# Two chained attentions on one core: other PSUM banks for the first attention's products, the next image's group statistics and several evictions moved in the written-out order, and two casts moved from VectorE to ScalarE

## Time and profile before

| | |
|---|---|
| median of 3 runs (lowest to highest) | 1849.27 us (1845.56 to 1850.44) |
| the profiled execution's own time | 1847.24 us |
| its span, first to last instruction | 1845.3 us |
| granted clock of TensorE, mean | 0.996 |
| PE / PEld busy | 95% / 86% |
| DVE / ACT / POOL busy | 76% / 51% / 41% |
| transfers | 169.67 MB, 92 GB/s over the span |

### The profile page before, as it was taken

The page is one execution under the profiler, slowest core; times in us unless marked ns, Lnnn a source line. Parts: engine busy times, 40 slices in busy tenths (PEclk is TensorE's granted clock), DMA queues, the critical chain, the costliest instruction groups (busy, mean ns, idle before and its releaser), DMA issues.

```text
span 1845.3 us, 34579 instructions
## 1 busy us (share of the span) xinstructions
PE 1760.7 (95%) x11810; PEld 1594.0 (86%) x11810; DVE 1403.4 (76%) x2596; ACT 937.6 (51%) x1476; POOL 754.1 (41%) x1334
## 2 busy tenths in 40 slices
PE   7999999999999999999999999999999999999997
PEld 6898888988889888898988989888898888988887
DVE  5778867787687877868778687786878868787675
ACT  3645545455463554635547354464545546456462
POOL 0442715327162361724617145271542715327161
PEclk9999999999999999999999999999999999999999
DMA  3404134051330504306042150422404134051330
GB/s 121 139 24 149 58 101 127 23 169 36 114 114 29 173 25 125 102 34 193 0 143 84 57 171 3 146 78 73 155 23 148 57 98 129 23 171 34 94 113 24
DMA packets 108575, 169.67 MB, mean 92 GB/s; under 512 B 12928, under 2 KB 79872, under 8 KB 108544
## 3 DMA queue, kind: packets, MB, share of 16 engines
q1 hardware_dynamic: 108544, 169.27, 29.0%
HBM read 85.33 MB, written 83.89 MB: 92 GB/s over the span
## 4 chain that ended last, share of the span: by engine, by line
PE 42%; issue 24%; POOL 21%; DVE 6%; ACT 4%; DMA 2%; POOLq 1%; SPq 1%; DVEq 0%; ACTq 0%
PE wide L368 12%; PE narrow L368 5%; POOL prob L1279 4%; PE wide L470 4%; PE wide L472 3%; PE wide L471 3%; PE narrow L470 3%; POOL ln_r L1247 3%; PE narrow L472 3%; PE narrow L471 3%; POOL sq_root L1261 2%; POOL ln_shift L1249 2%; PE turn L423 2%; PE turn L564 2%; PE turn L555 1%
## 5 line engine op out<-in xcount | busy, mean ns | idle before, releaser
L368 PE MATMUL wide<-xn_hi,prob 128*128 128x512 f32 x1024 | 304.9, 399 | 0.3 <-ACT expo L727 0.3
L1244 POOL TENSOR_TENSOR ln_v<-ln_mv,ln_eps 128x2 f32<-128x2 f32 (+2 forms) x128 | 39.2, 307 | 586.5 <-DVE ln_mv L1011 335.5
L761 ACT ACTIVATE ln<-tok,ln_shift,ln_r 128x256 f32<-128x256 f32 x128 | 68.4, 592 | 308.1 <-POOL ln_shift L1249 308.1
L368 PEld LDWEIGHTS wide<-xn_hi,prob 128*128 128x128 f32 x1024 | 185.5, 188 | 39.1 <-ACT expo L727 0.7
L727 ACT ACTIVATE expo<-wide,neg_max 128x1024 f32<-128x1024 f32 x128 | 142.1, 1110 | 136.2 <-DVE neg_max L983 136.2
L470 PE MATMUL narrow<-prob 128*128 128x256 f32 x640 | 188.6, 295 | 21.7 <-DVE tok L1006 18.6
L734 ACT ACTIVATE prob<-e_back 128x1024 fp32r<-128x1024 f32 x128 | 135.2, 1056 | 127.1 <-DMA e_back<-e_scratch 123.4
L990 DVE STREAM_TRANSPOSE x_norm<-expo 128x1024 f32<-128x1024 f32 x128 | 158.9, 1242 | 42.8 <-ACT expo L727 38.3
L471 PE MATMUL narrow<-prob 128*128 128x256 f32 x640 | 181.5, 284 | 0.0
L472 PE MATMUL narrow<-prob 128*128 128x256 f32 x640 | 181.4, 283 | 0.0
L1289 POOL TENSOR_TENSOR carrier_p<-ones 128x1 f32<-128x1 f32 x60 | 11.6, 193 | 415.5 <-DVE y_sb L1059 413.0
(11 more groups left out here) (182 smaller groups left out, 5392.8 us busy)
## 6 DMA issues: line engine op xcount, KB each, us to landing
e_scratch<-x_norm SPq DMA_DIRECT2D x128, 512.0 KB, 3.0
e_back<-e_scratch SPq DMA_DIRECT2D x512, 128.0 KB, 3.1
x_raw<-in_x SPq DMA_DIRECT2D x32, 512.0 KB, 3.9
out<-y_sb SPq DMA_DIRECT2D x32, 512.0 KB, 3.8
tok<-in_L_conv_qkv_w SPq DMA_DIRECT2D x1, 768.0 KB, 6.7
ln<-in_L_conv_proj_w SPq DMA_DIRECT2D x1, 256.0 KB, 6.8
ln<-in_L_ffn_weight SPq DMA_DIRECT2D x1, 256.0 KB, 3.9
out_bias<-in_L_conv_proj_b SPq DMA_DIRECT2D x1, 128.0 KB, 3.7
```

The costliest lines, as they stand in the source:

```text
L368: mm = pe.matmul(o, lhsT, r, start=first and i == 0, stop=last and i == len(parts) - 1)
L761: act.activation(ln2[:, n], tok[:, n], ACT.Identity, bias=ln2_shift[:, n:n + 1], scale=ln2_r[:, n:n + 1]).then_inc(ln2_made, 1)
```

## The change

The first attention's products no longer share one bank: blocks 0 to 3 go to narrow0, narrow1, narrow0 and the upper half of wide0, and the waits follow the banks. The group norm's two small products move from the turn tile to narrow0. On PE, `group_means` and `group_vars` move from the middle of the first attention to behind `turn_e2(2)` and `turn_e2(3)`, `scores1(7)`, `turn_cos(0)` and `product1(6)`, `product1(7)` move. On DVE, the two `gn_sums` move from the first attention to before and after `residual1(7)`, and `residual1`, `cosT_lo`, `e1T_lo`, `output` change places. On ACT, `exp2`, `cosT_hi`, `layer_norm1` change places; on POOL, `value_lo(1)` and `gn_coefficients` move back. The casts of the last row block of the second attention (two of 128x512 per image) are made by ACT behind the exponentials instead of by DVE. The number of matmuls, transfers and of all other operations stays.

```
-        out1 = [narrow[0]] * 4 + [turn[:, 0:BANK], narrow[0], wide[0][:, BANK:N], wide[1][:, BANK:N]]
-        gn_up = turn[:, BANK:BANK + KC]
+        out1 = [narrow[0], narrow[1], narrow[0], wide[0][:, BANK:N],
+                turn[:, 0:BANK], narrow[0], wide[0][:, BANK:N], wide[1][:, BANK:N]]
+        gn_up = narrow[0][:, 0:KC]
...
             def product1(b, n):
                 if n == 0:
                     pe.wait_ge(v_made, 4 * b + 4)
-                elif n < 4:
-                    pe.wait_ge(t1_made, NT * b + n)
-                elif n == 5:
-                    pe.wait_ge(t1_made, NT * b + 4)
+                elif n == 2:
+                    pe.wait_ge(t1_made, NT * b + 1)
+                elif n == 3:
+                    pe.wait_ge(e1_made, NT * b + 7)
+                elif n in (5, 6):
+                    pe.wait_ge(t1_made, NT * b + n - 2)
...
+                else:
+                    pe.wait_ge(t1_made, NT * b + 2)
...
                 product1(b, 2)
+                scores1(b, 7)
+                turn_cos(b, 0)
+                product1(b, 3)
...
-                if more:
-                    group_means(b + 1)
-                scores1(b, 7)
-                turn_cos(b, 0)
-                product1(b, 3)
                 product1(b, 4)
                 scores2(b, 0)
                 scores2(b, 1)
-                if more:
-                    group_vars(b + 1)
                 product1(b, 5)
+                product1(b, 6)
                 turn_cos(b, 1)
-                product1(b, 6)
-                if more:
-                    pe.wait_ge(gn_var, b + 2)
                 turn_e2(b, 1)
+                product1(b, 7)
                 scores2(b, 2)
-                product1(b, 7)
                 turn_cos(b, 2)
                 scores2(b, 3)
                 turn_e2(b, 2)
+                if more:
+                    pe.wait_ge(t1_made, NT * b + 6)
+                    group_means(b + 1)
                 scores2(b, 4)
                 turn_cos(b, 3)
                 turn_e2(b, 3)
+                if more:
+                    group_vars(b + 1)
                 scores2(b, 5)
+                turn_e2(b, 4)
                 turn_cos(b, 4)
-                turn_e2(b, 4)
...
                 turn_e2(b, 6)
+                if more:
+                    pe.wait_ge(gn_var, b + 2)
...
+            def e2_last_hi(b, u):
+                J, c0, c1 = PARTS[u]
+                act.wait_ge(e2_made, NP * b + u + 1)
+                act.activation(prob[:, 0, J, c0:c1], expo[:, J % DEEP, c0:c1], ACT.Copy).then_inc(p_last_hi_made, 1)
...
                 e1T_hi(b, 6)
-                layer_norm1(b, 1)
                 exp2(b, 0)
                 exp2(b, 1)
+                layer_norm1(b, 1)
                 unit_rows(b, 1)
-                cosT_hi(b, 1)
                 e1T_hi(b, 7)
                 layer_norm1(b, 2)
-                exp2(b, 2)
+                cosT_hi(b, 1)
                 unit_rows(b, 2)
                 layer_norm1(b, 3)
+                exp2(b, 2)
                 cosT_hi(b, 2)
                 unit_rows(b, 3)
                 exp2(b, 3)
                 layer_norm1(b, 4)
+                unit_rows(b, 4)
                 cosT_hi(b, 3)
-                unit_rows(b, 4)
...
                 exp2(b, 7)
+                e2_last_hi(b, 7)
                 exp2(b, 8)
+                e2_last_hi(b, 8)
...
                 residual1(b, 0)
-                if more:
-                    gn_sums(b + 1, 0)
                 row_max(b, 5)
                 e1T_lo(b, 2)
-                if f is not None:
-                    output(f, 1)
                 e1_turn(b, 5)
                 residual1(b, 1)
-                if more:
-                    gn_sums(b + 1, 1)
+                if f is not None:
+                    output(f, 1)
                 row_max(b, 6)
                 e1T_lo(b, 3)
                 e1_turn(b, 6)
-                residual1(b, 2)
                 row_max(b, 7)
                 e1T_lo(b, 4)
                 e1_turn(b, 7)
                 cosT_lo(b, 0)
+                e1T_lo(b, 5)
+                residual1(b, 2)
                 residual1(b, 3)
-                e1T_lo(b, 5)
-                if more:
-                    gn_deviation(b + 1)
+                e1T_lo(b, 6)
                 residual1(b, 4)
-                e1T_lo(b, 6)
-                if more:
-                    gn_variance(b + 1)
                 e2_hi(b, 0)
                 e2_hi(b, 1)
                 residual1(b, 5)
-                cosT_lo(b, 1)
                 e1T_lo(b, 7)
                 residual1(b, 6)
+                cosT_lo(b, 1)
+                if more:
+                    gn_sums(b + 1, 0)
                 e2T_parts(b, 1)
+                residual1(b, 7)
+                if more:
+                    gn_sums(b + 1, 1)
                 e2_hi(b, 2)
-                residual1(b, 7)
                 cosT_lo(b, 2)
                 e2T_parts(b, 2)
+                if more:
+                    gn_deviation(b + 1)
                 e2_hi(b, 3)
                 cosT_lo(b, 3)
                 e2T_parts(b, 3)
+                if more:
+                    gn_variance(b + 1)
                 e2_hi(b, 4)
+                e2T_parts(b, 4)
                 cosT_lo(b, 4)
-                e2T_parts(b, 4)
...
                 e2_hi(b, 6)
-                e2_hi(b, 7)
                 e2_last_lo(b, 7)
                 e2T_parts(b, 6)
-                e2_hi(b, 8)
                 e2_last_lo(b, 8)
...
-                value_lo(b, 1)
                 layer_norm1(b, 2)
                 lengths(b, 2)
+                value_lo(b, 1)
...
                 value_lo(b, 4)
-                if more:
-                    gn_coefficients(b + 1)
                 e2_lo(b, 4)
                 e2_lo(b, 5)
                 e2_lo(b, 6)
+                if more:
+                    gn_coefficients(b + 1)
```

More of the change, by code:

```diff
@@ L241, in build @@
         p_made = sem("p_made")
+        p_last_hi_made = sem("p_last_hi_made")
         p_last_made = sem("p_last_made")
@@ L1026, in e2_last_lo @@
                 J, c0, c1 = PARTS[u]
-                dve.wait_ge(p_hi_made, NP * b + u + 1)
+                dve.wait_ge(p_last_hi_made, 2 * b + u - NT + 2)
                 dve.tensor_sub(prob[:, 1, J, c0:c1], expo[:, J % DEEP, c0:c1],
@@ L1111, in front @@
                 residual1(b, 0)
-                if more:
-                    gn_sums(b + 1, 0)
                 row_max(b, 5)
                 e1T_lo(b, 2)
+                e1_turn(b, 5)
+                residual1(b, 1)
                 if f is not None:
                     output(f, 1)
-                e1_turn(b, 5)
-                residual1(b, 1)
-                if more:
-                    gn_sums(b + 1, 1)
                 row_max(b, 6)
@@ L1277, in e2_lo @@
                 row = slice(0, (J + 1) * P)
-                pool.wait_ge(p_hi_made, NP * b + J + 1)
+                pool.wait_ge(p_hi_made, (NT - 1) * b + J + 1)
                 pool.tensor_sub(prob[:, 1, J, row], expo[:, J % DEEP, row], prob[:, 0, J, row].bitcast(F32)
```

## The result

The changed kernel takes 1840.45 us (median of 8 runs, 1836.0 to 1844.7), the kernel before 1847.74 on the same chip (8 runs, 1844.41 to 1850.44). The ratio is 0.9962, with an interval of [0.9947, 0.9977]: 7 us less, and just over what a measurement here can tell from nothing. The profiled execution took 1838.84 us. The forecast of 1842 lies 1.6 us above the median. But the working behind it was only half right, and that is what this part is about.

The account below looks back on a forecast made before the run. PE, busy 95%, bounds the kernel, so only its waits can be won. Terms of 0.05 - 0.4 = -0.35 us per image, times 15, and -1.7 for the last image give -7: 1842 us, range 1838 to 1846.

Parts of the forecast that it names:

- Banks and block 7: First attention: `product1(3)` 1.7 us earlier; waits of 0.2 at `turn_cos(1)` and 1.8 at `product1(7)` give back 1.9.
- The late `ln_shift`: On POOL, group 2: DVE's `e1T_lo(7)` goes first by 0.1 us, so `ln_shift` ends at 988.4, not 987.5.
- the casts at nothing: Two ACT casts per image, 0.63 us each, lie beside PE and cost nothing; without that cover, 1.2 us per image.
- DVE with the statistics: Ahead of `scores2(4)`: moved statistics cost about 2.4 us of DVE's time ahead of PE; `scores2(4)` starts 0.8 late.
- From `scores2(4)` to `product2(0)`: Second attention: 11.95 us instead of 12.7; the 0.94 lost at `turn_e2(4)` goes, `group_vars` adds 0.2.
- Behind `product2(0)`: Inside `product2(0)`, 0.22 + 0.15 us go, as `gn_coefficients` now stand behind `e2_lo(6)` on POOL.
- The sum: Whole kernel: -0.35 us per image with a successor, times 15 = -5.3; last image -1.7; together -7 us.
- A: Rival: on POOL `ln_shift` gets through first, `cosT_hi(1)` comes 0.9 us earlier; -1.3 per image, 1828 us; chance 0.18.
- B: Rival: block 7's transfer lands late; at +0.9 an image loses 0.55 us instead of winning 0.35; 1856 us; chance 0.20.
- C: Rival: nothing gained; all PE stalls move and their sum stays, or the bank change frees nothing; 1849 us; chance 0.15.
- D: Rival: the chains are shorter than thought and most of the ceiling comes true; under 1825 us; chance 0.05.

Follow-up runs that it names:

- experiment 1: Kernel before with only the new `product1` banks and the waits that follow from them: 1848.37 us against 1848.94, ratio 0.9996.
- experiment 2: Changed kernel with the two casts of the last row block back on DVE: 1839.72 us, ratio 0.9954 to the kernel before.
- 3: Changed kernel with group 2's layer norm coefficients ahead of `e2_lo(0)` and `e2_lo(1)` on POOL: 1842.27 us, ratio 0.9974 to the kernel before.
- 5: Changed kernel with `cosT_hi(1)` back ahead of `layer_norm1(2)` on ACT: 1839.65 us, ratio 0.9949 to the kernel before.
- 6: As 5, with `exp2(2)` also ahead of `layer_norm1(3)` on ACT: 1838.4 us, ratio 0.9947 to the kernel before.
- 7: As 6, with `cosT_lo(2)` ahead of the cast `e2_hi(2)` on DVE: 1829.93 us, ratio 0.9896 to the kernel before.
- 8: As 6, DVE's order untouched, with POOL's `value_lo(2)` behind the small operations of group 4: 1831.35 us, ratio 0.9907 to the kernel before.
- 4: Changed kernel with `e1T_hi(7)` ahead of `unit_rows(1)` on ACT: 1839.31 us, ratio 0.995 to the kernel before.
- 10: Changed kernel with 11 idle matmuls ahead of `product1(7)`, where PE waits 1.45 us: 1838.2 us, ratio 0.9944 to the kernel before.
- 11: As 7, with 11 idle matmuls filling PE's wait ahead of `product1(7)`: 1824.32 us, ratio 0.9868 to the kernel before.
- 12: As 11, with `gn_sums(1)` behind `cosT_lo(2)` and `e2_hi(2)`, and `group_means` behind `scores2(4)`: 1824.98 us, ratio 0.9869 to the kernel before.

## Why the prediction was right, and where only its sum was

- *Banks and block 7: right.* The bank change frees 1.2 us at one place and block 7's chain takes it back: `product1(7)` was forecast to a tenth. Its split into two waits was off (0.2 and 1.8 foreseen, 0.89 and 1.45 found), without effect on the end. Two small errors cancel in it: `product1(3)`, at whose end the chain begins, started at 51.6 us of the image instead of 51.9 and ended half a us sooner than worked out, and the way from there to block 7 took that much longer. In experiment 1, where the order is the old one, other waits take the 1.2 us.
- *The late `ln_shift` and the casts at nothing: right*, by the rows of after and by experiment 2.
- *DVE with the statistics: sized too high, and taken for the only bound.* "2.4 of DVE's time ahead of PE" made `scores2(4)` 0.8 late on image 8; in image 9 of after it is 76.33 - 75.72 = 0.6 later than in image 8 of before, and on average over the images at full clock 76.20 - 75.96 = 0.2. The smaller operations taken at 0.9 together were 0.8. What the step missed altogether are two bounds a few tenths behind: the cast's meeting with `value_lo(2)`, and the same `value_lo(2)` ahead of group 4's coefficients, for which `exp2(4)` and `turn_e2(4)` wait. That is why 3, 5 and 6, which take away the first, win no time (0.2 us at most in an image at full clock), why 7, which takes away the second as well, makes such an image no shorter than 6, and why 8 does.
- *From `scores2(4)` to `product2(0)`: the saving sized too low.* 11.95 us forecast, 11.74 measured at full clock, 12.72 before. The wait of 0.78 at `turn_e2(4)` is gone, as foreseen.
- *Behind `product2(0)`: sized too low as well.* The image won 24.64 - 23.97 = 0.7 us, where the step had 0.37. All of it is in the first block of `product2`: 3.65 us from its start to the next one's before, 2.98 after. Beside the wait of 0.22 three smaller stumbles in this block are gone. After has this gain, experiment 2 has it too and experiment 1 has not, so it comes from the moves and not from the casts or the banks; that it is the `gn_coefficients` moved back, as predicted, was not tested alone.
- *The clock: not in the working.* The working has no term for it. The eight drops take back 0.7 us per image on average.
- *The sum met its time by luck.* An image at full clock gained 113.08 - 112.04 = 1.0 us (image 8 of before, image 9 of after), and on average 113.24 - 111.91 = 1.3, where the forecast was 0.35; the clock took 0.7 of it back, and 113.24 - 112.65 = 0.6 us per image is left over the 14 images between the first and the last. The last image won 133.04 - 131.97 = 1.1 us (1.7 forecast), and image 1 starts 0.9 us later than before, within what the start of these kernels varies by. That makes the 8.5 us between the two spans; the medians differ by 7.3. So a forecast of -7 agrees with the measurement because a gain three times too small met a loss that it did not have.
- *Rivals.* A did not happen in the change, and when forced its earlier `cosT_lo(1)` won nothing (3). B did not: the fetch of block 7 went at 1088.15, 3.54 us behind its send at 1084.61 and not 4.7, and ACT never waited for it in the loop; 4 shows that the room was about 1 us. C holds for the banks alone. D, times below 1825, needed three more moves and the fill.

Left open: which of the moves brings which part. The places where the image got shorter, `turn_e2(4)` and the first block of `product2`, are read from the traces; no run takes back one of these moves by itself.

## What to carry to other kernels

When a wait goes at one place of hand-ordered queues, look for the second and third bound behind it, and above all for short copies and casts on VectorE that stand ahead of something TensorE wants while GpSimd runs a long subtraction. Here either side paid for such a meeting, up to nearly the whole length of the other's instruction. Moving the critical operation ahead (7) and moving the opponent (8) both cleared it, but only the second also freed what stood behind the opponent in its own list. So judge a move by the length of the image and not only by the place that it was meant for. And on a TensorE that is 96% busy, compare images at full clock with one another: if images alternate between two durations, look at the granted clock, and try to fill or part the waits ahead of its drops.

## What the runs showed that I had not expected

- The clock of TensorE falls to its lower level in a kernel whose TensorE is 96% busy, behind waits none of which is over 1.5 us. A drop costs nothing (image 8 of after), 0.7 us (7), 1.5 us (after) or 2.5 us (8), by what waits it removes or adds behind it.
- Neither total nor longest wait tells whether it falls: images of 10 wait 2.2 us, at most 0.8 at once, and every second one has a drop; those of 11 wait as much, at most 0.9 at once, and those of 12 2.4, with 1.25 at once, and none has. In 10 three waits lie within 2.1 us just ahead of the drop (74.2 to 76.2); what decides is not shown.
- Idle matmuls that replace a wait of 1.45 us won 5 us over a kernel in which the wait itself stayed as long.
- A cast of 128x384 took 0.33 us or 1.36 in images of the same run (6), as it got ahead of GpSimd's subtraction of 1.18 or not.
- The time after a change can agree with its forecast to a tenth of a per cent while four of its terms are off by 0.2 to 0.7 us per image.
